# Zeroing by DMA, keys before queries, the first maxima before the values, and spare matmuls between the MoE and the second attention

## What is computed

```python
b, s, _ = x.shape                     # 1, 2048; x is normed and modulated
q = (x @ Wqa @ Wqb).reshape(b, s, 16, 8)
kv = (x @ Wkva @ Wkvb).reshape(b, s, 4, 8, 2)
k, v = (kv[..., 0], kv[..., 1])
q, k = _rope(q), _rope(k)             # each key head serves 4 query heads
scores = einsum('bqhd,bkhd->bhqk', q, k) * scale
w = softmax(where(causal, -inf, scores), axis=-1)
out = einsum('bhqk,bkhd->bqhd', w, v).reshape(b, s, 128) @ Wout + bout
```

## Time and profile before

| what | before |
|---|---|
| median of 3 runs | 1230.65 us (1227.99 to 1236.67) |
| the profiled execution | 1230.85 us, of which the span is 1229.0 |
| PE busy | 1099.2 us, 89% of the span |
| DVE busy | 928.7 us, 76% |
| ACT busy | 742.2 us, 60% |
| POOL busy | 186.8 us, 15% |
| end of the MoE's last product to the first step of the second pass | 418 to 485 us |

### The profile page before, as it was taken

How to read it: one execution, slowest core, us unless ns; L and a number is a source line. 1 busy time by engine, 2 the same in 40 slices (tenths; PEclk the granted TensorE clock), 3 DMA queues, 4 the chain that set the end, 5 groups by cost and what they waited for, 6 DMA issues and landing times.

```text
span 1229.0 us, 18062 instructions
## 1 busy us (share of the span) xinstructions
PE 1099.2 (89%) x5956; PEld 613.7 (50%) x5971; DVE 928.7 (76%) x1803; ACT 742.2 (60%) x1088; POOL 186.8 (15%) x144
## 2 busy tenths in 40 slices
PE   3897668899999677999999999999996999999998
PEld 2333235577777523333333232222225788888886
DVE  5599998455655576799899999999606788888885
ACT  2635426688788522445566666666784666666664
POOL 0000001499899900100000000000000000000000
PEclk9999777899999876999999999999995899999999
DMA  6000001799997314200000000000000211111001
GB/s 172 1 0 1 1 0 48 158 203 203 209 202 172 132 26 97 51 2 2 2 1 2 1 1 2 1 2 1 1 1 1 97 60 60 60 60 60 1 1 35
DMA packets 39521, 65.44 MB, mean 53 GB/s; under 512 B 14622, under 2 KB 30782, under 8 KB 34126
## 3 DMA queue, kind: packets, MB, share of 16 engines
q1 hardware_dynamic: 39446, 64.43, 21.5%
HBM read 61.17 MB, written 3.11 MB: 52 GB/s over the span
## 4 chain that ended last, share of the span: by engine, by line
PE 62%; DVE 26%; ACT 5%; issue 4%; POOL 2%; DMA 1%; SPq 0%; DVEq 0%; POOLq 0%; ACTq 0%
PE ps L929 10%; PE ps L930 10%; PE ps L931 10%; PE ps L1142 9%; PE ps L1071 7%; DVE arena_b L1902 6%; PE ps L1120 5%; DVE arena_b L1649 3%; PE ps L1127 2%; POOL parts L741 2%; PE ps L1084 2%; DVE arena_b L1830 1%; PE ps L791 1%; DVE arena_b L1663 1%; ACT arena_b L1462 1%
## 5 line engine op out<-in xcount | busy, mean ns | idle before, releaser
L1462 ACT ACTIVATE arena_b<-ps 128x1024 f32<-128x1024 f32 (+3 forms) x320 | 273.8, 894 | 154.2 <-PE ps L1120 130.6
L929 PE MATMUL ps<-parts 128*128 128x512 f32 x640 | 253.2, 396 | 10.1 <-POOL parts L741 7.6
L930 PE MATMUL ps<-parts 128*128 128x512 f32 x640 | 250.0, 391 | 0.0
L931 PE MATMUL ps<-parts 128*128 128x512 f32 x640 | 249.8, 390 | 0.0
L1902 DVE TENSOR_REDUCE arena_b<-ps 128x1 f32<-128x512 f32 x384 | 238.3, 681 | 9.8 <-PE ps L1071 8.4
L1071 PE MATMUL ps<-arena_a 48*128 48x512 bf16 (+7 forms) x820 | 179.0, 311 | 12.8 <-DVE arena_b L1902 4.5
L741 POOL TENSOR_TENSOR parts<-arena_b,parts 128x512 fp32r<-128x512 f32 x128 | 166.7, 1311 | 62.7 <-ACT parts L1392 58.1
L1142 PE MATMUL ps<-arena_b 128*32 128x512 f32 (+3 forms) x1280 | 151.1, 544 | 0.0
L1830 DVE SCALAR_TENSOR_TENSOR arena_b<-ps,arena_a 128x512 f32<-128x512 f32 x128 | 87.0, 688 | 80.5 <-PE ps L931 80.4
L1120 PE MATMUL ps<-arena_a 50*128 50x512 bf16 (+3 forms) x832 | 139.3, 311 | 7.9 <-DMA arena_a<-arena_b 4.0
L1071 PEld LDWEIGHTS ps<-arena_a 48*128 48x128 bf16 (+1 forms) x832 | 60.3, 96 | 170.7 <-DVE arena_b L1902 104.7
(11 more groups left out here) (270 smaller groups left out, 1140.1 us busy)
## 6 DMA issues: line engine op xcount, KB each, us to landing
arena_a<-root_weights SPq DMA_DIRECT2D x60, 512.0 KB, 6.6
arena_b<-expert_weights SPq DMA_DIRECT2D x7, 1024.0 KB, 6.1
arena_a<-q_parts SPq DMA_DIRECT2D x36, 64.0 KB
wslot<-in_L_ffn_up_w SPq DMA_DIRECT2D x8, 256.0 KB, 7.0
wslot<-in_L_ffn_down_w SPq DMA_DIRECT2D x8, 256.0 KB, 7.6
wslot<-in_L_ffn_w_gate SPq DMA_DIRECT2D x8, 256.0 KB, 2.9
wslot<-in_L_ffn_w_up SPq DMA_DIRECT2D x8, 256.0 KB, 3.2
wslot<-in_L_ffn_w_down SPq DMA_DIRECT2D x8, 256.0 KB, 3.8
```

Source lines behind the costliest of these rows:

```text
L929: mm(bank, w(0), x(0), start=start, stop=False)
L930: mm(bank, w(0), x(1), start=False, stop=False)
L931: return mm(bank, w(1), x(0), start=False, stop=stop)
L1462: a(probs[:, s % 2, 2 * pair:2 * pair + 2, off:CW], ps[:, 2 + 2 * pair:4 + 2 * pair, off:CW], ACT.Exp, scale=scale).then_inc(p2_exp, 1)
```

## The change

- **Zeros.** POOL's two fills go. SP loads zeros from a DRAM row instead, five DMAs behind the rotary tables and ahead of the first FFN weights: 78 and 64 and 14 partitions of 16 KB in `kst`, twice 16 partitions of 24 KB in `qst`, 3.34 MB in all. Only rows that nothing else fills are written. All waits for `kzero` become waits for `ld_zero`.
- **Projections.** PE's order after each turn becomes keys(0), queries(0), keys(1), keys(2), keys(3), queries(1), queries(2).
- **First maxima.** "maxima" of item 0 closes a `SLOTS[0]` of 16 slots, ahead of `queries(3)` and `values_all`. The four diagonal blocks of item 1 move beside step 0; steps 0 and 1 now have 10 slots each where they had 8. From `SLOTS[3]` on the slots are as before.
- **Rotary.** `rope_q` is cut in two multiplications (`rope_mult`) and the rest (`rope_rest`, five instructions, which ends in `split_ready`). For chunks 2 and 3 the multiplications come ahead of step 0, and the rest behind the slots beside step 1 and step 3.
- **Spare matmuls.** PE multiplies an identity matrix by itself into a bank that nobody reads: 8 behind the second turn of the MoE's sum, 14 behind the fourth, 8 behind the first turn of the layernorm, 16 ahead of the stacks, and one behind each of eight slots of `SLOTS[0]`.
- The values go through bank 6, and the wait for them moves into step 1.

```diff
@@ attention_schedule
+        if n == 1:
+            scores.append(("maxima", 0))
         for k, (what, t, u) in enumerate(blocks):
             scores += [(what, n, t, u, i) for i in range(HPG)]
-            if k == 0 and n > 0:
+            if k == 0 and n > 1:
                 scores.append(("maxima", n - 1))
@@ SP
             sp.dma_start(ropek, A["ropek"].rearrange("p (a t) -> p a t", a=2)).then_inc(ld_rope, 16)
+            sp.wait_ge(moe_prod, N_IT0 * MU)
+            zeros = A["zeros"]
+            for rows, half in ((slice(MROWS, P), 0), (slice(0, STRIP), 1), (slice(STRIP + MROWS, P), 1)):
+                sp.dma_start(kst[rows, half].rearrange("p g t -> p (g t)"),
+                             zeros[:, 0:G1 * T].broadcast_to([rows.stop - rows.start, G1 * T])).then_inc(ld_zero, 16)
+            for rows in (slice(KROWS, STRIP), slice(STRIP + KROWS, P)):
+                sp.dma_start(qst[rows, 1:NC].rearrange("p c g a t -> p (c g a t)"),
+                             zeros.broadcast_to([STRIP - KROWS, QZERO])).then_inc(ld_zero, 16)
             for slot in range(2):
                 load1(slot, slot)
...
-                sp.wait_ge(kzero, 1)
+                sp.wait_ge(ld_zero, ZEROED)
...
-                sp.wait_ge(qzero, 1)
                 sp.wait_ge(st_q[c], 16)
@@ POOL
-            pool.wait_ge(moe_down, N_IT0 * MU)
-            pool.wait_ge(moe_prod, N_IT0 * MU)
-            g.memset(kst[:, :, :, :].rearrange("p h g t -> p (h g t)").bitcast(F32), 0.0).then_inc(kzero, 1)
-            g.memset(qst[:, 1:NC].rearrange("p c g a t -> p (c g a t)").bitcast(F32), 0.0).then_inc(qzero, 1)
@@ PE
                 last.then_inc(y0_tr, 1)
+                if c == 1:
+                    pe.wait_ge(y0_ready, NC)
+                    for _ in range(8):
+                        mm(ps[:, 7, :], identb[:, :], identb[:, :].unsqueeze(1).broadcast_to([P, TPC, P]), start=True, stop=True)
+                if c == NC - 1:
+                    for _ in range(14):
+                        mm(ps[:, 7, :], identb[:, :], identb[:, :].unsqueeze(1).broadcast_to([P, TPC, P]), start=True, stop=True)
+            def warm(count, bank=7):
+
+                for _ in range(count):
+                    mm(ps[:, bank, :], identb[:, :], identb[:, :].unsqueeze(1).broadcast_to([P, TPC, P]), start=True, stop=True)
...
             def values_all():
 
-                pe.wait_ge(rope_done, 6)
                 for t in range(NT):
-                    last = mm(ps[:, 4, t * 32:(t + 1) * 32], hT[:, PAD + t * P:PAD + (t + 1) * P], wkv[:, 2, :],
+                    last = mm(ps[:, 6, t * 32:(t + 1) * 32], hT[:, PAD + t * P:PAD + (t + 1) * P], wkv[:, 2, :],
                               start=True, stop=True)
...
             def after_turn(c):
 
-                if c >= 1:
-                    if c <= 2:
-                        queries(c - 1)
+                if c == 0:
+                    warm(8)
+                else:
                     keys(c - 1)
+                    if c == 1:
+                        queries(0)
...
                 pe.wait_ge(p2_exp, 2 * s + 2)
+                if s == 0:
+                    pe.wait_ge(v_ready, 1)
...
             keys(NC - 1)
+            queries(1)
             queries(2)
+            warm(16, 0)
             stacks_before()
-            for what in SLOTS[0][:NITEM0]:
+            for what in SLOTS[0]:
                 slot(what)
+                if what[0] in ("diag", "below3"):
+                    warm(1)
             queries(3)
             values_all()
-            for what in SLOTS[0][NITEM0:]:
-                slot(what)
-            pe.wait_ge(v_ready, 1)
             pe.wait_ge(rope_done, 2 * NC)
@@ DVE
-            def rope_q(c):
+            def rope_mult(c):
...
                 v.tensor_tensor(rb[:, b, :], ps[:, bank + 1, :], ropes[:, chunk(c)], ALU.mult).then_inc(rope_done, 1)
+
+            def rope_rest(c):
+
+                b = c % 2
                 dve.wait_ge(rope_done, 2 * c + 2)
...
-            rope_q(0)
+            rope_mult(0)
+            rope_rest(0)
             rope_k()
-            rope_q(1)
-            for what in SLOTS[0][:NITEM0]:
+            rope_mult(1)
+            rope_rest(1)
+            for what in SLOTS[0]:
                 slot(what)
-            rope_q(2)
-            for what in SLOTS[0][NITEM0:]:
-                slot(what)
-            rope_q(3)
+            rope_mult(2)
+            rope_mult(3)
             for s in range(len(STEPS)):
                 for what in SLOTS[s + 1]:
                     slot(what)
+                if s in (1, 3):
+                    rope_rest(2 + s // 2)
@@ _constants
+        "zeros": np.zeros((1, QZERO), np.uint16),
```

More of the change, by code:

```diff
@@ L46 @@
 MROWS = KROWS + 2
+QZERO = (NC - 1) * G1 * 2 * CW
+ZEROED = 16 * 5
 STRIP = 64
@@ L458, in adaln_two_layers @@
         assert [x[2:] for x in ORDER if x[0] == "stack"] == STACKS[PRE:]
-        NITEM0 = min(k for k, x in enumerate(SLOTS[0]) if x[1] == 1 or x[0] == "maxima")
         def light(s):
@@ L1438, in _ @@
                 stack_copy(e, 6 + e % 2)
-            slots(SLOTS[0][:NITEM0])
+            slots(SLOTS[0])
             act.wait_ge(v_mm, 1)
             act.wait_ge(vzero, 2)
-            a(vaug[:, :, :, 0:HD], ps[:, 4, :].rearrange("p (n g d) -> p n g d", g=G1, d=HD), ACT.Copy)\
+            a(vaug[:, :, :, 0:HD], ps[:, 6, :].rearrange("p (n g d) -> p n g d", g=G1, d=HD), ACT.Copy)\
                 .then_inc(v_ready, 1)
-            slots(SLOTS[0][NITEM0:])
             def copy_out(n, steps):
```

10 lines of the change are left out of this document (6 added, 4 removed).

## The result

The changed kernel took 1246.88 us in the median (1242.77 to 1256.61, 4 runs), the kernel before 1229.32 us beside it (1227.23 to 1236.67, 4 runs). The ratio is 1.0125, with a 95% interval from 1.008 to 1.017: slower, by about 15 us, with 10 and 21 us as the bounds.

What follows compares the result with a forecast made beforehand. Bounds seen: POOL's fills holding DVE (7.0 us), PE's half clock, queued loads ahead of step 0. Sum: -5.9 at step 0, +13.3 to step 4, +2.0 clock: +9.4, forecast 1240 us; own range 1233 to 1245, with rivals 1227 to 1247.

Steps and rivals of the forecast that it cites:

- main term: Between step 0 and step 4: the row of item 1 comes late, +13.3 us (32.3 instead of 19.0).
- rival of the late zeros: Zeros on SP's queue take over 20.9 us, step 0 at 486, time 1246 us and more; chance 0.13.
- part 1: MoE's end to the keys: without POOL's fills DVE saves 7.0 us, key stores can begin at 444.5 instead of 453.51.
- part 2: SP's queue: zeros take 18.0 us (8.1 to 20.9), key loads begin at 451.2, step 0 5.9 us sooner.
- second wait: Ahead of step 4: PE waits about 10 us for the row of item 1.
- part 3: Step 0 to step 4: row of item 1 waits behind chunk 2's split and query loads; 32.3 us, step 4 at 511.5.
- late row: Row of item 1 on SP, behind `stack_q(2)` and its 12 loads; PE waits 10 us for it.
- part 4: PE behind the wait ahead of step 4: half clock costs 2 us, bounds 0 and 4.
- Spare matmuls hold the clock: PE from 418 to 440: full clock, keys ready 9.0 us sooner; the rival that it fails, 1245 us, chance 0.05.
- The move of the maxima gains nothing: Steps 0 and 1: nothing waits for the first maxima; the four moved diagonal blocks make step 1 2.5 us later.
- rival of the early row: Step 4: the row of item 1 is in time, so no second wait; -2 us, 1229 us, chance 0.22.

Runs made afterwards that it cites:

- e12: Kernel before, with only POOL's two fills cut into 28 pieces of 512 columns; 1228.76 us, ratio to the kernel before 0.9968.
- e3: Changed kernel with zeros written by POOL's two fills again instead of five DMAs; no time given, attention ends 525.7 us after the MoE's end (changed kernel 531.9).
- e4: Changed kernel without any spare matmul; no time given, attention ends 530.7 us after the MoE's end (changed kernel 531.9).
- e1: Changed kernel, but SP writes the row of item 1 ahead of the second query loads; 1236.58 us, ratio to the kernel before 1.0027.
- e2: Changed kernel with rope_rest of chunks 2 and 3 back ahead of step 0; no time given, attention ends 517.6 us after the MoE's end (changed kernel 531.9).
- e10: e9 without the spare matmuls; no time given, attention ends 518.4 us after the MoE's end (e9 517.7).
- e11: e9 with the first maxima again behind the four diagonal blocks of item 1, ahead of step 0; 1215.97 us in one execution.
- e6: e1 with zeros written by POOL in 28 fills of 512 columns, none by DMA; 1219.38 us in one execution.
- e9: e6 again, the same program, timed in 12 runs; median 1231.12 us, ratio to the kernel before 0.9968.
- e7: e6 with the row of item 0 also ahead of the store and loads of query chunk 1; 1227.87 us, ratio to the kernel before 0.9926.
- e8: e7 without spare matmuls; no time given, attention ends 509.0 us after the MoE's end (e7 506.9).
- e5: e1 with zeros loaded to all 128 partitions, 7.34 MB instead of 3.34; no time given, attention ends 516.6 us after the MoE's end (e1 514.6).

## Why the prediction was right, and where it was wrong

The forecast was 1240 us, slower than before, with a range from 1227 to 1247; measured were 1246.9. The sign and the main term hold. The size was too small by nearly half, and for one step the mechanism was a rival's. That 1246.9 lies inside the range is luck: it is beyond the forecast's own 1233 to 1245, and a tenth of a microsecond below an upper end that was taken from the rival of the late zeros.

- **DVE's hold and the keys (part 1): right.** Stores at M+24.9, forecast 26.2. e12 gives the hold alone: 7.2 us at the attention's end.
- **The zeros (part 2): this step failed.** I took 18.0 us, with 20.9 as the upper bound. The first window's 352 GB/s for 8 us, 2.8 MB, are the tables; from 434 to 458.3 it was 24.3, beyond the bound. The wide zeros moved at 207 GB/s as taken, but only for 7 us; then came stretches of 139, 183 and 117. The trace's DMA packets can be told apart by size: 16 KB are the rows of `kst`, 24 KB those of 16 partitions in `qst`, 2 KB and 512 B the weights. The 16 KB packets, 2.57 MB, went from 433.6 to 450.4, at 153 GB/s on average where I had 208. The 24 KB ones began at 439.3 among them and ended at 457.0; while they had the queue nearly to themselves, from 450 to 454, they moved at 92 to 99 GB/s, where I had 150. Beside them went weights, and the last of the weights was through at 462.4, M+36.5, where I had M+30.4. The key stores, queued behind them, landed 10.1 to 11.3 us after they were issued, and the loads began 1.2 us behind the last weight. Key loads came 1.0 us sooner than before, not 5.9. The Trainium skill, "SBUF — State Buffer", section "Door 1: The DMA port swizzle", gives about 109 GB/s for 16 neighbouring partitions. The trace has 92 to 99, near it, and the page's was the better value than my 150. By the prediction's estimate from it, it accounts for 2.5 of the 5.9 us by which the zeros landed late. The rest is the wide zeros among others on the queue, for which nothing here gives a rule.
- **This made the second rival come true as well**: "the zeros are late" named 20.9 us of zeros as the point from which it decides, step 0 at 486 and a time from 1246 us on. Step 0 was at M+67.5, which is 485.8 on the old trace's clock, though by the landing of what was queued and not by late stores, as it had it. Its condition of mixed loads below 208 GB/s held, that of narrow ones below 70 did not. I had given it 0.13 as an alternative; it came on top of the second wait.
- **From step 0 to step 4 (part 3): right, and 3.8 us short of this trace for the clock alone.** e3 and e4, which have the same late row and 5.6 and 5.9 us of half clock, take 32.7 and 32.0 us where I had 32.3. The changed kernel's trace has 36.1. The pieces: 19.8 us to the copy of the second maxima (step 0 at 493.35, `rope_rest(2)` from 513.28) where I had 16.4; 3.0 for the five instructions (3.1); 2.3 for the store (2.8); 10.8 from the first load to step 4 (10.0). e1 and e2 show that it is the late row. It costs 8 to 12 us by traces with like clocks and some 12 by the ratios, not the 17.3 and 14.3 of the bare positions; I had it stand for 10.
- **The clock (part 4): in the wrong place.** I put 2 us behind the second wait. The half clock came there too (0.50 from 529.4 to 537.0), but behind step 4 there was only 0.6 us to pay (18.4 - 0.6 - 17.2). What cost more lay behind the first wait: 0.50 for 16.4 us from step 0 on, where I had read some 7 us off, and this is what made 16.4 into 19.8 in this trace; in e3 and e4 it did not come.
- **The sum**: +0.6 at step 0 (forecast -5.9), +17.2 to step 4 (+13.3), +0.6 behind it (+2.0): +18.4, forecast +9.4. The measured difference of the medians is 17.6 us.
- **"Spare matmuls hold the clock": right, and no gain is shown.** It was full from 426 to 458, but the attention ends 1.2 us sooner without them in e4 and 0.6 us later in e10, with clocks that differ behind step 0 as well.
- **"The move of the maxima gains nothing": right**; its price, 2.5 us in the sum and 2.9 in the rival of the early row, was too high: e11 has 1.1 us in the steps, given back ahead of step 0.

## What to carry to other kernels

An instruction moved to a later place on one engine moves every semaphore that it sets: look up which in-order queue waits for it, and what of another stage stands behind on that queue; here five DVE instructions, 3 us of work, cost some 12 us through SP. Work taken off an engine and put on a DMA queue is not free, and bytes to few partitions were the dearest here: count what is issued behind it. And measure from a common point near the change, since the same program can be 7 us off upstream and 10 us off in a race between two engines. Even then look at the clock stretch by stretch before you put the difference of two traces down to an edit: here 3 to 5 us of it were the length of one stretch of half clock.

## What was not expected of the hardware

- **One program, two outcomes between POOL and DVE.** With 28 short fills on POOL (13.1 to 13.9 us together) DVE's 128x4 tensor_scalar lasted 0.35 us in e6 and 9.70 us in e9, from the same start. Of seven traces with pieces four were free (e6, e7, e11, e12) and three held (e8, e9, e10). POOL's own time tells them apart: 13.88 to 13.90 us where DVE got in, 13.12 to 13.13 where it didn't. With one long fill in place of the pieces, as before and in e3, both traces were held.
- **Half clock outlasts its wait, and by very different times.** Behind the 13.2 us wait of the changed kernel it stayed for 16.4 us with PE busy for 15.62 of them, in e5 for 16.6 us with 15.65; behind the like waits of e3, e4, e1 and e2 it was over after 4.7 to 5.9 us. Behind step 0 of e7 the average was 0.52 for 16.9 us with no wait at all ahead; in e6, behind 5.7 us, it was 0.77 for 7.3 us and full from then on.
- **SP is held while it issues.** Two weight loads took 6.85 and 7.40 us to issue in the changed kernel where others on that queue took about half a microsecond; in e5 three took 6.34, 4.22 and 7.23. It cost nothing here, since the key stores came later still.
- **The same 12 key loads drain in 13.8 to 20.1 us** (from the first load to the first query load behind them: e6 13.8, after 18.2, e4 and e2 20.1). No row here says why, and it is as large as some terms of the sum.
